# A fused attention and expert kernel: weight loads issued from ScalarE, reciprocal roots by GpSimd powers, and a new order of all engines' lists

## The reference

```
def _layernorm(x, axis=-1, eps=1e-05):
    m = jnp.mean(x, axis=axis, keepdims=True)
    v = jnp.var(x, axis=axis, keepdims=True)
    return (x - m) / jnp.sqrt(v + eps)
...
    attn = jnp.einsum('bhdq,bhdk->bhqk', qh, kh)
    attn = jax.nn.softmax(s * attn, axis=-1)
    out = jnp.einsum('bhqk,bhdk->bhdq', attn, vh)
...
    logits = x_flat @ w_router.T
    probs = jax.nn.softmax(logits, axis=-1)
    top_idx = jnp.argmax(probs, axis=-1)
    h = jnp.einsum('nd,ehd->enh', x_flat, w_fc)
    a = jnp.square(jnp.where(h >= 0, h, 0.5 * h))
    expert_out = jnp.einsum('enh,edh->end', a, w_proj)
...
    x = x + _L0_xcond_ref(_layernorm(x, axis=-1), ctx_2048, ctx_2048, itok_B_779_1933)
    x = x + _L0_ffn_ref(_layernorm(x, axis=-1), L0_ffn_w_router, L0_ffn_w_fc, L0_ffn_w_proj)
```

## Time and profile before

| | before |
|---|---|
| time of the runs | 173.63 us median (172.86 to 173.75, 3 runs) |
| span of the profiled execution | 170.4 us |
| PE, DVE, ACT, POOL busy | 161.4, 129.2, 97.0, 58.6 us |
| granted TensorE clock, mean | 0.999 of full speed |
| instructions | 4075 |

### The profile page before, as it was taken

The page is one execution under the profiler, slowest core; times in us unless marked ns, Lnnn a source line. Parts: engine busy times, 40 slices in busy tenths (PEclk is TensorE's granted clock), DMA queues, the critical chain, the costliest instruction groups (busy, mean ns, idle before and its releaser), DMA issues.

```text
span 170.4 us, 4075 instructions
## 1 busy us (share of the span) xinstructions
PE 161.4 (95%) x1494; PEld 139.9 (82%) x1494; DVE 129.2 (76%) x301; ACT 97.0 (57%) x181; POOL 58.6 (34%) x68
## 2 busy tenths in 40 slices
PE   7998887899999989999989999999999999999992
PEld 7986745487698869896978798969879999999991
DVE  7799987999898999995999867953179875056442
ACT  4444979558659956957346526943794065335220
POOL 7331544630322420372521260405023253136330
PEclk9999999999999999999999999999999999999999
DMA  4577857794468054004501460002010000010001
GB/s 120 167 241 246 259 190 233 217 292 126 143 229 251 3 161 120 14 19 139 174 0 62 125 189 4 0 0 67 0 62 0 4 0 0 4 61 0 0 4 62
DMA packets 18883, 16.98 MB, mean 100 GB/s; under 512 B 1776, under 2 KB 18672, under 8 KB 18864
## 3 DMA queue, kind: packets, MB, share of 16 engines
q1 hardware_dynamic: 18144, 16.00, 30.3%
q10 hardware_dynamic: 720, 0.73, 1.5%
HBM read 8.72 MB, written 1.05 MB: 57 GB/s over the span
## 4 chain that ended last, share of the span: by engine, by line
PE 75%; DVE 11%; issue 4%; SPq 3%; ACT 3%; DMA 2%; DVEq 0%; ACTq 0%
PE hp L1358 25%; PE ops L1388 22%; PE pv L1342 6%; PE stp L1318 6%; PE ops L1273 5%; DVE negm L813 5%; PE snp L1265 3%; DMA x_raw<-x 2%; ACT probs L514 2%; DVE a_lo L921 2%; PE ops L1376 2%; PE pv L1376 1%; PE stp L1324 1%; PE pv L1398 1%; PE snp L1301 1%
## 5 line engine op out<-in xcount | busy, mean ns | idle before, releaser
L378 POOL TENSOR_TENSOR a_buf<-l_buf 128x512 f32<-128x512 f32 x32 | 35.7, 1119 | 77.8 <-DVE a_lo L921 44.6
L514 ACT ACTIVATE probs<-stp,scale_b 128x1024 f32<-128x1024 f32 x30 | 33.4, 1114 | 14.8 <-PE stp L1318 11.3
L1358 PE MATMUL hp<-xt_hi,wfc_hi 128*128 128x256 f32 x128 | 37.2, 291 | 0.0
L813 DVE TENSOR_REDUCE negm<-snp 128x4 f32<-128x1024 f32 x28 | 34.1, 1218 | 3.6 <-PE snp L1265 3.4
L1358 PE MATMUL hp<-xt_hi,wfc_lo 128*128 128x256 f32 x128 | 35.8, 279 | 0.0
L1358 PE MATMUL hp<-xt_lo,wfc_hi 128*128 128x256 f32 x128 | 35.7, 279 | 0.0
L522 ACT ACTIVATE l_buf<-hp 128x512 f32<-128x512 f32 x32 | 18.8, 594 | 23.7 <-PE hp L1358 17.0
L921 DVE TENSOR_TENSOR a_lo<-a_buf,a_hi 128x512 fp32r<-128x512 f32 x32 | 26.2, 831 | 7.6 <-ACT a_hi L529 6.2
L1358 PEld LDWEIGHTS hp<-xt_hi,wfc_hi 128*128 128x128 f32 x128 | 24.0, 188 | 2.1 <-issue 1.0
L1388 PE MATMUL ops<-wproj_hi,a_hi 128*128 128x256 f32 x112 | 23.6, 292 | 0.5 <-DVE wproj_lo L953 0.5
L1358 PEld LDWEIGHTS hp<-xt_hi,wfc_lo 128*128 128x128 f32 x128 | 24.1, 188 | 0.0
(11 more groups left out here) (112 smaller groups left out, 237.2 us busy)
## 6 DMA issues: line engine op xcount, KB each, us to landing
k_st<-k_hi SPq DMA_DIRECT2D x16, 128.0 KB, 2.1
wfc_raw<-w_fc_t SPq DMA_DIRECT2D x8, 256.0 KB, 4.4
wproj_raw<-w_proj_t SPq DMA_DIRECT2D x8, 256.0 KB, 3.5
q_st<-q_hi SPq DMA_DIRECT2D x14, 128.0 KB, 2.1
x_raw<-x SPq DMA_DIRECT2D x8, 128.0 KB, 3.0
k_st<-k_lo SPq DMA_DIRECT2D x8, 128.0 KB, 2.4
v_raw<-ctx_t SPq DMA_DIRECT2D x8, 128.0 KB, 2.6
x_keep<-x SPq DMA_DIRECT2D x8, 128.0 KB, 2.7
```

The lines of the kernel that those rows point to most:

```text
L378: pool.tensor_tensor(a_buf[d % 2][:, :, :], l_buf[d % 2][:, :, :], l_buf[d % 2][:, :, :], ALU.mult).then_inc(s_a, 1)
L514: act.activation(probs[g][:, :, :, :], pair[:, :, :].rearrange("p e (c n) -> p e c n", c=KC), ACT.Exp, scale=scale_b[:, b:b + 1]).then_inc ...
L813: dve.tensor_reduce(negm[b % 2][:, :, :, g].rearrange("p c e -> p e c"), pair[:, :, :].rearrange("p e (c n) -> p e c n", c=KC), AX.X, ALU. ...
L1358: last = pe.matmul(hp[:, d % 2, half], wfc[w][:, kc, c * P:(c + 1) * P], xt[:, kc, :], start=(c % 2 == 0 and kc == 0 and w == 0 and xt is ...
```

## The change

Three things are changed, and no work of the FFN or the attention is added or taken away.

1. All 16 `load_weights` go from SP's list to ACT's list, and `load_consts` goes ahead of the loads of the context there.
2. The reciprocal root is one POOL instruction, a power with the exponent -0.5 from a tile that DVE fills once (`fill_expo`). `x_moments(b, 2)` gives variance + eps, and waits for the power two batches back. `x_ln`, `x_rstd`, `y_ln`, `y_rstd`, `x_newton` and `x2_newton` are gone.
3. The lists of all five engines are in a new order.

```
-                    dve.tensor_scalar(var[:, :], mv[:, 1:2], EPS, -0.5, ALU.add, ALU.mult).then_inc(s_var_, 1)
+                    wait(dve, s_used, b - 1)
+                    dve.tensor_scalar(var[:, :], mv[:, 1:2], EPS, None, ALU.add).then_inc(s_var_, 1)
...
+            def x_scale(b):
+                j = b % 2
+                if b == 0:
+                    pool.wait_ge(s_expo, 1)
+                pool.wait_ge(s_xvar, b + 1)
+                wait(pool, s_qf, b - 1)
+                pool.tensor_tensor(xsc[j][:, :], xvar[j][:, :], expo[:, :], ALU.pow).then_inc(s_xsc, 1)
...
+            def y_scale(b):
+                j = b % 2
+                pool.wait_ge(s_yvar, b + 1)
+                wait(pool, s_x2n, b - 1)
+                pool.tensor_tensor(ysc[j][:, :], yvar[j][:, :], expo[:, :], ALU.pow).then_inc(s_ysc, 1)
...
-            load_weights(sp, 0, 0)
...
+            load_weights(act, 0, 0)
```

More of the change, by code:

```diff
@@ L87, in build @@
         yst, ymv, yvar = two("yst", [P, 6]), two("ymv", [P, 2]), two("yvar", [P, 1])
-        yln, yrs, yn1, ysc = (two(n, [P, 1]) for n in ("yln", "yrs", "yn1", "ysc"))
+        ysc = two("ysc", [P, 1])
         dot_out = sb("dot_out", [P, DIM])
@@ L410, in _ @@
             square(0, 2)
+            split_k(5)
+            place_v(4)
             square(0, 3)
-            split_k(5)
             square(0, 4)
+            x_scale(6)
+            x_scale(7)
+            y_scale(2)
+            y_scale(3)
             square(0, 5)
-            place_v(4)
             square(0, 6)
+            square(0, 7)
             split_k(6)
-            square(0, 7)
+            square(1, 0)
             place_v(5)
+            place_v(6)
             split_k(7)
-            square(1, 0)
-            place_v(6)
             square(1, 1)
@@ L426, in _ @@
             square(1, 4)
+            place_v(7)
+            y_scale(4)
+            y_scale(5)
             square(1, 5)
@@ L435, in _ @@
             square(2, 4)
+            y_scale(6)
+            y_scale(7)
             square(2, 5)
@@ L987, in _ @@
             split_max_lo(0)
+            q_part_lo(1)
+            len_scale()
             x_moments(2, 0)
@@ L1061, in _ @@
+            split_max_lo(3)
+            q_part_lo(5)
+            x_moments(6, 2)
             x_moments(7, 0)
             x_moments(7, 1)
+            router(0)
+            split_w_lo(1, 0)
             square_lo(0, 0)
             router(1)
-            split_max_hi(3)
-            split_w_lo(1, 0)
-            split_max_lo(3)
+            square_lo(0, 1)
+            split_w_lo(1, 1)
+            row_max(4, 0)
             pv_turn(2)
+            den_inverse(2)
+            row_max(4, 1)
@@ L1100, in _ @@
-            x2_newton(2, 0)
-            x2_newton(2, 1)
+            x2_sum(2)
+            x2_moments(2, 0)
+            row_max(4, 3)
+            split_max_hi(4)
+            pv_turn(3)
+            split_max_lo(4)
+            den_inverse(3)
+            split_w_lo(1, 4)
+            coef_sum(0)
+            attention_out(3)
+            square_lo(0, 3)
+            x_moments(7, 2)
+            q_normalise(6)
+            attention_turn(3)
+            x2_moments(2, 1)
+            top_weight(0)
@@ L1128, in _ @@
+            split_w_lo(1, 7)
+            row_max(6, 0)
+            q_part_lo(7)
+            square_lo(1, 0)
             pv_turn(4)
-            square_lo(0, 6)
-            split_w_lo(1, 6)
-            square_lo(0, 7)
             den_inverse(4)
+            row_max(6, 1)
+            coef_sum(1)
+            square_lo(1, 1)
+            row_max(6, 2)
+            expert_out(0, 1)
             attention_out(4)
-            split_w_lo(1, 7)
-            router(3)
+            top_weight(1)
@@ L1427, in _ @@
             warm(21)
-            scores_qk(0, 2)
             warm(22)
             warm(23)
-            scores_qk(0, 3)
             warm(24)
+            max_transpose(0)
+            scores_kq(0, 0)
             warm(25)
@@ L1455, in _ @@
             max_transpose(1)
+            warm(32)
+            warm(33)
             scores_kq(1, 0)
+            scores_kq(1, 1)
+            warm(34)
+            fill(3)
             warm(35)
-            scores_kq(1, 1)
             scores_qk(2, 0)
@@ L1484, in _ @@
             scores_qk(3, 1)
+            x_transpose(0)
             warm(48)
-            x_transpose(0)
+            warm(49)
             scores_kq(2, 2)
             scores_qk(3, 2)
-            warm(49)
             ffn1(0, 0)
```

772 lines of the change are left out of this document (331 added, 441 removed).

## The result

The changed kernel takes 174.11 us (median of 10 runs, 173.24 to 177.82), the kernel before 172.72 beside it (10 runs, 172.33 to 173.75): a ratio of 1.0073 with a 95% interval of 1.005 to 1.0096. So it is slower by 0.7%, which is clear of the interval but small. The profiled execution has a span of 171.6 us and 173.53 in all; before, the span was 170.4.

A forecast was written before the change was run, and what follows sets the result against it. Bound: start of `x_transpose(0)`, set by batches 0 to 2's attention, then PE's work and stalls, plus 3.6 us of tail. Terms -0.1 + 1.2 - 0.7 = +0.4 gave span 170.8, time 174.0; range 172.3 to 176.5.

The forecast's parts named there:

- q of batch 0: Early start: `q_f` of batch 0 begins at 5.95 instead of 5.04 us, behind POOL's first power, 0.9 later.
- The first call: POOL's first power: setup between 0 and 0.98 us, taken as 0, against the skill's about 6 us.
- rival (d): POOL's first power pays the skill's 6 us for a freshly loaded library: 6.4 us more, time 180; chance 0.05.
- `x_transpose(0)` at 39.7: First step of the FFN: starts at about 39.7 instead of 39.83 us, -0.1 (-0.5 to +1.9).
- nothing on the path: The 16 issues added on ACT: 1.5 us in all there (0 to 9), none of it delaying the critical path.
- DVE's work from `row_max(2,0)` to `x_transpose(0)`: Last stretch before the FFN, limited by DVE: falls from about 11.9 to about 11.1 us.
- PE's work behind it: PE after `x_transpose(0)`: runs of FFN chunks broken 33 times instead of 27, 0.2 us each, +1.2 (0.6 to 1.6).
- stalls: PE's idle times after `x_transpose(0)`: about 2 us before, a third of it goes, -0.7 (-2.0 to +2.5).
- (b): Power of 1.28 us plus 0.98 for a first call delays POOL, paid twice: +2.4, 176.0; chance 0.15.
- (a): DVE's relief pays in full: `x_transpose(0)` at 39.2 and PE's idle times after it vanish, -1.4, 172.2; chance 0.22.
- (c): New waits of 2.5 us where PE is full, from POOL's `y_scale` and ACT's splits: +2.1, 175.7; chance 0.15.
- One sign of being wrong: PE's stretch after `x_transpose(0)` shorter than 126 us or longer than 129.5 would show the forecast wrong.

The follow-up runs named there:

- splits moved: Changed kernel with POOL's weight split (0,6) ahead of the copy of v of batch 2 and split (0,7) behind the first square: 172.88 us, ratio to before 0.9997.
- the loads behind `q_put`: Changed kernel with ACT's first three weight loads after q_put, their splits later, and some POOL calls reordered: 179.79 us, ratio to before 1.038.
- the addresses of before: Changed kernel plus an unused tile of 352 bytes per partition, putting xt and a back at their old addresses, no instruction changed: 175.44 us, ratio to before 1.0163.

## Why the prediction was right in its number and wrong in its steps

**The number.** 174.0 was forecast, 174.11 measured, and that is luck twice over. The forecast stood on 173.63, the median of three runs of the kernel before; the ten runs beside the changed kernel have 172.72, and with them the same sum, +0.4, would have given 173.1, 1.0 too low. And the sum was of terms that were wrong and cancelled. Measured side by side the change is slower by 0.7%, not no change; that had a chance of 0.35.

**q of batch 0** (+0.9 forecast): +0.2. Cst, first in its queue, was there at 2.76 and not at 3.75, which gave back more than the power's longer duration took (0.57 instead of 0.3). (Its old wait ended 3.75 behind its issue, 5.22 - 1.47, and not 3.6.)

**The first call.** No gap of microseconds stands ahead of the first power, so rival (d) fell. The 6 us that the Trainium skill (GPSIMD Engine Reference, Instruction dispatch) gives for a first call into freshly loaded code did not show here.

**`x_transpose(0)` at 39.7**: this step failed, it came at 42.78. Starts in the traces, in us:

| | before | changed | later by | splits moved |
|---|---|---|---|---|
| first scores of batch 0 | 8.07 | 9.81 | 1.74 | 9.85 |
| `max_transpose(0)` | 14.04 | 15.45 | 1.41 | 15.48 |
| `row_max(2,0)` | 27.89 | 29.14 | 1.25 | 29.17 |
| `max_transpose(2)` | 35.58 | 36.59 | 1.01 | 36.62 |
| first scores of batch 3 | 37.19 | 38.85 | 1.66 | 38.36 |
| `x_transpose(0)` | 39.83 | 42.78 | 2.95 | 40.83 |

The working followed the instructions of each engine and left out two things that the same lists show. The weight loads were priced as issue time on ACT ("nothing on the path"), not by their packets: the queue that carries them takes 73% of the DMA engines while k_st of batch 0 is stacked, 13% without them. That is 1.5 us at the first scores, by the loads behind `q_put`. About 1.0 of it is left at `max_transpose(2)` and, with the splits moved, at `x_transpose(0)`. And POOL's work was costed only as something in the way of POOL, not of DVE: 1.46 us at x2n, by the moved splits, and 0.5 more at the scores of batch 3. These wait 0.61 us for the landing of q_st, and why that DMA lands late was not tested.

DVE's work from `row_max(2,0)` to `x_transpose(0)` was forecast to fall from 11.9 to 11.1 us. (The terms given, -0.9, -0.75 and +0.5, make it 10.75.) It took 13.64, 12.18 without the collision at x2n, and 11.66 with the splits moved. So the relief on DVE, on which that step rested, shows as 0.3 us there, with the landing of q_st in the way.

**PE's work behind it, +1.2, and stalls, -0.7**: together +0.5, measured -1.69. PE's busy time is in the windows from `x_transpose(0)` to the last matmul, of the kernel before, the changed one, and the changed one with the addresses of before:

```profile
39.83:166.78 126.95, 125.72 (x1173) 111.86 (x1172) 93.56 (x210) 72.35 (x130) 40.76 (x40) 1.00 0.21 63
```

```profile
42.78:168.04 125.26, 124.82 (x1173) 110.93 (x1174) 92.03 (x194) 69.92 (x114) 44.01 (x47) 1.00 0.21 61
```

```profile
42.77:169.31 126.54, 126.43 (x1173) 112.53 (x1174) 92.49 (x194) 69.91 (x114) 43.91 (x47) 1.00 0.20 61
```

PE's idle time is what is left: 1.23, 0.44 and 0.11 us. (The ends of matmuls are modelled in a profile, so these are estimates.) The stalls were 1.23 and not 2, and fell by 0.79, about as forecast. With the addresses of before PE is busy for 0.71 longer, so the six more interruptions cost about 0.12 each and not 0.2. The term that the sum did not have is the pace: at the new addresses the same matmuls take 1.61 less, which no step could see in a list. -0.79 + 0.71 - 1.61 = -1.69.

**The rivals and signs.** (b), the power in POOL's way, was to decide from a power of 0.8 us; it was 0.57, and most of the loss goes with the two splits. Where a power was in the way it was by its place in the list. (a) asked for a start 0.6 earlier. (c) put the new stalls into the full part; they were ahead of it. One sign of being wrong came: PE's stretch behind `x_transpose(0)` is 125.26, under 126. The clock was in no case, with 0.4 us of the median.

## What to carry to other kernels

Read a new order for what runs at the same time on DVE and POOL and on the DMA queues, not only for what stands ahead of what: two POOL calls beside two DVE steps cost 1.46 us here, half of the 2.8 us of instructions that the change takes off DVE ahead of them. The loads issued from ACT were free in issue time only; look at whose packets are under way when a DMA on the path is issued. And when tiles are added or taken away, compare the pace of a long run of equal matmuls in both traces before anything else, since it may have changed without any instruction changing.

## What was not expected of the hardware

The pace of 128x256 matmuls with 32-bit operands depends on where the tiles lie in SBUF: 115.3 to 119.6 ns from start to start for the same list of PE, with shifts of 64 to 352 bytes, some 670 times 4 ns between the ends. Four DVE steps that take 0.41 us elsewhere took 1.34 to 1.36 where they began 0.07 to 0.23 us behind the start of a POOL subtraction of 1.26 to 1.45 us. And one idle time of PE of 1.77 us was followed by a stretch at half the clock in one execution of a kernel whose other profile, with a shorter idle time there (0.61 us), had none.
